# Adaptive layer norm, state-space mixing and routed feed-forward on one core: setup reordered, the weight fetches put one behind the other, the router's bias added on VectorE

## The reference

```
h   = layernorm(x) * (1 + ca) + sa
S_t = a * S_(t-1) + (1 - a) * h_t                # a = sigmoid(decay_logit), per channel
x   = x + ga * (S @ W.T + b + conv5(h) + conv_b)
h   = layernorm(x) * (1 + cb) + sb
logits = gelu(h[last token] @ Wp1 + bp1) @ Wp2 + bp2
e   = argmax(softmax(logits))                    # one of 8 experts for the whole row
x   = x + gb * (h + 0.3 * ((gelu(h @ W1[e] + b1[e]) @ W2[e] + b2[e]) @ Wo + bo))
```

## Time and profile before

| | us |
|---|---|
| median of 3 runs | 666.33 (662.33 to 667.11) |
| the profiled execution | 664.8 |
| its span, first to last instruction | 662.8 |
| PE busy | 640.0 (97% of the span) |
| DVE busy | 561.0 (85%) |
| ACT busy | 562.2 (85%) |
| POOL busy | 447.6 (68%) |
| TensorE's mean granted clock | 0.996 of full |

### The profile page before, as it was taken

One profiled execution on the slowest core, in us unless ns is written; L12 is line 12 of the kernel. 1 busy time (PEld: TensorE's weight loads), 2 busy tenths in 40 slices (PEclk: granted clock), 3 DMA queues, 4 the chain that ended last, 5 costly groups with the idle time before them and its releaser, 6 DMA issues.

```text
span 662.8 us, 11162 instructions
## 1 busy us (share of the span) xinstructions
PE 640.0 (97%) x3469; PEld 526.8 (79%) x3469; DVE 561.0 (85%) x863; ACT 562.2 (85%) x976; POOL 447.6 (68%) x536
## 2 busy tenths in 40 slices
PE   6988999999999999999999999999999999999986
PEld 6877778888888878888888888888888878888765
DVE  1697889999999989999999999999999989998612
ACT  3788688889988888888998889888899889887753
POOL 2885476876667666777676766778776766666543
PEclk9999999999999999999999999999999999999999
DMA  8999546665555554665454555566555445555551
GB/s 288 357 349 319 162 128 192 191 186 149 156 159 180 159 183 167 192 192 179 124 194 149 182 161 186 164 191 191 189 143 153 150 167 188 160 159 159 159 158 65
DMA packets 55454, 120.58 MB, mean 182 GB/s; under 512 B 5643, under 2 KB 43364, under 8 KB 46180
## 3 DMA queue, kind: packets, MB, share of 16 engines
q1 hardware_dynamic: 51844, 115.65, 54.9%
q10 hardware_dynamic: 3552, 4.23, 2.1%
HBM read 61.12 MB, written 25.19 MB: 130 GB/s over the span
## 4 chain that ended last, share of the span: by engine, by line
PE 82%; DMA 8%; ACT 3%; DVE 3%; issue 2%; POOL 1%; SPq 1%; DVEq 0%; ACTq 0%
PE U L1051 10%; PE U L1053 8%; PE U L1052 8%; PE Q L1071 8%; PE TR L1091 8%; PE Q L1066 8%; PE Q L1067 8%; DMA up_w<-up_table 5%; PE Q L1083 4%; PE Y L1035 4%; PE Y L1031 4%; PE Y L1032 4%; PE TR L1083 4%; PE Q L1016 2%; DMA xr<-in_L_ffn_W_dram 2%
## 5 line engine op out<-in xcount | busy, mean ns | idle before, releaser
L454 POOL TENSOR_TENSOR g_lo<-g,g_hi 128x512 fp32r<-128x512 f32 x128 | 169.8, 1329 | 151.5 <-ACT g_hi L614 149.4
L835 DVE SCALAR_TENSOR_TENSOR Y<-h,taps,Y 128x512 f32<-128x512 f32 x320 | 222.4, 750 | 3.2 <-PE Y L1035 0.9
L1051 PE MATMUL U<-hid_hi,up_w 128*128 128x512 f32 x256 | 110.1, 430 | 4.7 <-DMA up_w<-up_table 3.7
L1066 PE MATMUL Q<-g_hi,down_w 128*128 128x512 f32 x256 | 103.7, 405 | 0.3 <-issue 0.3
L566 ACT ACTIVATE S<-xr,nmr,rstd 128x256 f32<-128x256 f32 x128 | 66.6, 591 | 42.2 <-POOL S_lo L462 40.0
L1067 PE MATMUL Q<-g_hi,down_w 128*128 128x512 f32 x256 | 101.1, 395 | 0.0
L1053 PE MATMUL U<-hid_lo,up_w 128*128 128x512 f32 x256 | 100.8, 394 | 0.0
L1052 PE MATMUL U<-hid_hi,up_w 128*128 128x512 f32 x256 | 100.6, 393 | 0.0
L783 DVE BATCH_NORM_STATS2 st<-xr 128x6 f32<-128x512 f32 x128 | 88.0, 709 | 12.8 <-DMA xr<-in_L_attn_x_dram 8.5
L880 DVE TENSOR_TENSOR_SCAN S<-keep,h 128x512 f32<-128x512 f32 x64 | 76.6, 1235 | 25.3 <-ACT h L684 25.3
L607 ACT ACTIVATE g<-U,up_w 128x512 f32<-128x512 f32 x128 | 87.2, 682 | 10.8 <-PE U L1053 10.3
(11 more groups left out here) (116 smaller groups left out, 1272.3 us busy)
## 6 DMA issues: line engine op xcount, KB each, us to landing
up_w<-up_table SPq DMA_DIRECT2D x32, 1027.0 KB, 6.6
down_w<-down_tab SPq DMA_DIRECT2D x32, 1024.0 KB, 8.6
xr<-in_L_attn_x_dram SPq DMA_DIRECT2D x32, 512.0 KB, 3.5
out_dram<-xr SPq DMA_DIRECT2D x64, 256.0 KB, 2.3
xr<-in_L_ffn_W_dram ACTq DMA_DIRECT2D x5, 512.0 KB, 10.2
xr<-in_L_ffn_W_dram SPq DMA_DIRECT2D x4, 512.0 KB, 8.9
up_table<-g_lo SPq DMA_DIRECT2D x2, 1024.0 KB, 11.8
up_table<-down_w SPq DMA_DIRECT2D x2, 1024.0 KB, 13.4
```

The source lines that it names most:

```text
L454: nc.gpsimd.tensor_tensor(g_lo[:, f], g[:, f % 2], g_hi[:, f].bitcast(f32), ALU.subtract).then_inc(g_lo_ready, 1)
L835: ins = nc.vector.scalar_tensor_tensor(out=Y[c][:, :], in0=h[:, c, k:k + T], scalar=taps[:, c, k:k + 1], in1=Y[c][:, :], op0=ALU.mult, op1 ...
L1051: mm(U[f % 2][:, :], up_w[:, par, UP + w:UP + w + P], hid_hi[:, par, c], start=(c == 0), stop=False)
L1066: mm(Q[c][:, :], down_w[:, par, 1, w:w + P], g_hi[:, f], start=(f == 0), stop=False)
```

## The change

1. The router's bias leaves TensorE: `router_logits` is a single product, and VectorE adds the bias from PSUM into a new tile `logits`, with a wait of its own, before `max` and `max_index`.
2. In `fetch`, SyncE waits until `up_w` has landed before it issues `down_w`.
3. In TensorE's slot, `to_channels(i + 3)` moves ahead of `router_logits(i + 1)`, and `down(i, 1)` moves ahead of `up(i, 3)`.
4. ScalarE's slot has `gelu(i, 1)` ahead of `g_high(i, 0)`, and `g_high(i, 3)`, `s_high(i + 3, 0)`, `s_high(i + 3, 1)`, `gate2(i)` in this order at its end. GpSimd's has `gate_beta(i)` first.
5. All five setup lists are put in another order. SyncE no longer waits there for the modulation weights, and issues W2[0] and W ahead of the first x.

```diff
--- before.py
+++ after.py
@@ fetch, on SyncE
                 if r == 0:
                     sp.wait_ge(s_down_lo, 2 * E)
+
+                sp.wait_ge(up_loaded[par], 16 * (r // 2 + 1))
                 sp.dma_start(down_w[:, par].rearrange("p k n -> p (k n)").bitcast(f32),
@@ setup, on SyncE
             def prologue():
                 vectors()
+                load_w2(0)
+                load_w()
                 load_x(0)
-                load_w2(0)
+                load_wo()
                 load_taps()
-
-                for_modulations()
+                load_router()
                 load_w1(0)
...
                 split_out(3)
+                split_out(4)
+                beta_out()
...
@@ router, on VectorE
             def router(r):
                 dve.wait_ge(r_logits, r + 1)
-                nc.vector.max(top8[:, :], U[1][0:1, 8:8 + E]).then_inc(top_ready, 1)
+                if r == 0:
+                    dve.wait_ge(s_small, SMALL_LOADED)
+                nc.vector.tensor_tensor(logits[:, :], U[1][0:1, 8:8 + E], bp2_sb[:, :], ALU.add).then_inc(logits_ready, 1)
+                dve.wait_ge(logits_ready, r + 1)
+                nc.vector.max(top8[:, :], logits[:, :]).then_inc(top_ready, 1)
                 dve.wait_ge(top_ready, r + 1)
-                nc.vector.max_index(sel8[:, r % 2], top8[:, :], U[1][0:1, 8:8 + E]).then_inc(sel_ready, 1)
+                nc.vector.max_index(sel8[:, r % 2], top8[:, :], logits[:, :]).then_inc(sel_ready, 1)
@@ slot, on ScalarE
                 if row(i):
                     gelu(i, 0)
+                    gelu(i, 1)
                     g_high(i, 0)
-                    gelu(i, 1)
                     g_high(i, 1)
@@ router_logits, on TensorE
                 pe.wait_ge(nav_ready, r + 1)
-                mm(U[1][0:1, 8:8 + E], nav[:, :], wp2[:, :], start=True, stop=False)
-                mm(U[1][0:1, 8:8 + E], ident[0:1, 0:1], bp2_sb[:, :], start=False, stop=True).then_inc(r_logits, 1)
+                mm(U[1][0:1, 8:8 + E], nav[:, :], wp2[:, :], start=True, stop=True).then_inc(r_logits, 1)
@@ slot, on TensorE
                     up(i, 2, (1,))
+                if row(i + 3):
+                    to_channels(i + 3, xn1, xn1_ready, t1_done)
                 if row(i + 1):
                     router_logits(i + 1)
-                if row(i + 3):
-                    to_channels(i + 3, xn1, xn1_ready, t1_done)
                 if row(i):
+                    down(i, 1)
                     up(i, 3)
                 if row(i + 2):
                     back_to_tokens(i + 2)
                 if row(i):
-                    down(i, 1)
                     down(i, 2)
                     down(i, 3)
```

More of the change, by code:

```diff
@@ L119, in adaln_attention_ffn_kernel @@
         nav = sb("nav", [P, 1])
+        logits = sb("logits", [1, E])
         top8 = sb("top8", [1, 8])
@@ L312, in vectors @@
                     sp.dma_start(dst, src).then_inc(s_vecs, 16)
-            def for_modulations():
-                for n in range(NMOD - 1):
-                    sp.wait_ge(s_wmod[n], 16 * DC)
             def load_w():
@@ L687, in prologue @@
             def prologue():
+                w2T_copy(0)
                 xn1_of(0)
                 w1_hi(0)
-                w2T_copy(0)
-                w1_hi(1)
-                mix_high()
                 h_of(0)
                 down_high(0, 0)
+                down_high(0, 1)
+                mix_high()
                 w2T_copy(1)
                 s_high(0, 0)
-                down_high(0, 1)
+                s_high(0, 1)
+                w1_hi(1)
+                down_high(1, 0)
                 w1_hi(2)
+                xn1_of(1)
+                w2T_copy(2)
                 w1_hi(3)
[L700 to L703, removed]
                 down_high(1, 1)
                 w1_hi(4)
-                w1_hi(5)
[L707 to L713, removed]
+                w2T_copy(3)
+                down_high(2, 0)
+                h_of(1)
+                down_high(2, 1)
+                gate1(0)
+                s_high(1, 0)
+                w2T_copy(4)
+                down_high(3, 0)
+                w1_hi(5)
+                w1_hi(6)
+                down_high(3, 1)
                 s_high(1, 1)
-                w2T_copy(4)
-                w1_hi(6)
                 w2T_copy(5)
-                down_high(3, 1)
+                xn1_of(2)
                 down_high(4, 0)
-                xn1_of(2)
-                w1_hi(7)
                 xn2_of(0)
@@ L725, in prologue @@
                 w2T_copy(6)
+                w1_hi(7)
                 down_high(5, 0)
-                hid_high(0)
[L728 to L735, removed]
-                down_high(6, 1)
+                gate1(1)
+                h_of(2)
+                down_high(5, 1)
+                w2T_copy(7)
+                down_high(6, 0)
+                down_high(6, 1)
+                nav_of(0)
+                s_high(2, 0)
+                s_high(2, 1)
+                hid_high(0)
                 down_high(7, 0)
@@ L910, in prologue @@
                 down_low(3, 1)
+                conv(1, 0, 6)
                 down_low(4, 0)
-                conv(1, 0, 6)
                 down_low(4, 1)
                 conv(1, 6, 10)
+                down_low(5, 0)
+                down_low(5, 1)
                 scan(2, 0)
-                down_low(5, 0)
                 scan(2, 1)
+                stats1(3)
+                down_low(6, 0)
+                down_low(6, 1)
+                router(0)
                 residual1(1, 0)
-                down_low(5, 1)
-                down_low(6, 0)
-                stats1(3)
-                router(0)
-                down_low(6, 1)
                 residual1(1, 1)
+                s_low1(2)
                 down_low(7, 0)
                 down_low(7, 1)
-                s_low1(2)
             def slot(i):
```

79 lines of the change are left out of this document (37 added, 42 removed).

## The result

The changed kernel took 683.92 us (median of 4 runs, 683.06 to 684.94) against 665.2 us for the kernel before (662.33 to 667.11): ratio 1.030, 95% interval 1.026 to 1.033. It is 3% slower, outside the range of the prediction and on its other side. The profiled execution has a span of 681.3 us (before 662.8), its mean granted clock 0.999 of full speed.

What follows compares the result with a forecast made beforehand. TensorE was taken as the bound; 7.5 + 0.5 + 1.4 + 1.8 + 0 + 0.7 - 0.4 = 11.5 us off the profiled 664.8 gave 653.3, moved half way toward the median's 1.5 us excess: 654 us, range 645 to 663.

Steps and rivals of the forecast that it cites:

- The step that failed: Steady slot: TensorE, busy all 18.40 us, sets its length; VectorE, with 1.3 us to spare, is next.
- The slower rival: `g_lo` of `up(i, 3)` comes late in every slot, 0.70 us of wait each; 674 us, chance 0.09.
- 4.7 us to spare: GpSimd's spare time in a steady slot, given as the argument against `g_lo` coming late.
- Bias and transposes, 0.25 us a slot: TensorE between `up(i, 2)` and the next large matmul: saving of 0.13 to 0.42 us, taken as 0.25.
- The term of 7.5 us: Bias product and moved transposes over all slots: 29 x 0.25 + 2 x 0.13 us saved, range 3.9 to 12.4.
- the first rival: VectorE becomes the bound; slot stays 18.4 us, 661 or 662 us in all, chance 0.15.
- Index: TensorE's two waits for the router's index go, as six matmuls now stand in between: gain 0.5 us.
- Fetch, 1.4 + 1.8 us: `up_w` lands some 1.7 us earlier: 1.4 us of waits in the middle saved, 1.8 in the tail.
- Setup, 0: Reordered setup lists gain nothing: `down(0, 0)` starts at 80.1 against 79.96.
- its wait of 0.70: Slot 0: TensorE's wait for `g_lo` goes, since TensorE stands still before and the others catch up; gain 0.7 us.
- Clock: Slot 0: 0.4 us taken off for the chance that TensorE's pauses make the granted clock fall.

Runs made afterwards that it cites:

- e2: Kernel before with only `gelu(i, 1)` moved ahead of `g_high(i, 0)`: 688.2 us, ratio 1.037.
- e9: Kernel before with 0.54 us of unused extra work on GpSimd ahead of `norm1` in each slot: 688.6 us, ratio 1.035.
- f7: Changed kernel with each slot's scans replaced by multiply-adds reading one operand from SBUF, one from PSUM (computes something else): 659.2 us, ratio 0.993.
- e3: Changed kernel with TensorE's slot back in the old order: 684.0 us, ratio 1.029.
- e7: Kernel before with only the router's bias moved to VectorE: 669.2 us, ratio 1.007.
- e6: Kernel before with only the wait of `down_w`'s fetch for `up_w` added: 661.5 us, ratio 0.995.
- f3: Kernel before with the fetch wait and all of the change's reordered setup: 660.0 us, ratio 0.995.
- e4: Changed kernel with `norm1(i + 4)` moved behind `g_low(i, 2)` on GpSimd: 701.0 us, ratio 1.056.
- f1: Changed kernel with row i + 4's statistics and `norm1` moved to the start of the slot: 686.3 us, ratio 1.034.
- f4: Kernel before with the fetch wait, and row i + 4's statistics and `norm1` moved to the start of the slot: 679.1 us, ratio 1.022.
- f8: f3 with only the power of `norm1` left on GpSimd, its other instructions on VectorE: 670.0 us, ratio 1.010.
- f5: Changed kernel with only the power of `norm1` left on GpSimd, its other instructions in the slots on VectorE: 660.4 us, ratio 0.995.

## Why the prediction was wrong

**The step that failed** is the first one: "a slot lasts as long as its TensorE instructions take to start one after the other", carried over to a slot of 18.15 us with the lengths of GpSimd's and VectorE's instructions unchanged. GpSimd's slack was read as time it could be late by. It was not that: in the trace of before, the negation of `norm1` passed ahead of the scan by 0.21 us, and where it does not, the instructions do not keep their lengths. The trace of the kernel before had the whole collision in it. In slot 0 the scan starts ahead of the negation (84.89 against 85.10):

```profile
85.10 1.04 POOL L438 TENSOR_SCALAR nmr<-st 128x4 f32<-128x4 f32 x1
86.11 1.96 POOL L440 TENSOR_TENSOR rstd<-rstd,minus_half 128x4 f32<-128x4 f32 x1
```

The wait of 0.70 us for `g_lo` and the slot of 19.41 us come behind it. The page had the power as a mean of 1193 ns for the group; taken one by one, it lasts 1.04 or about 2.0 us.

**The slower rival** had the sign (674 us; measured 684), the wait (line 1075, each slot, 0.55 us where it took 0.70) and even the edit, `gelu(i, 1)` ahead of `g_high(i, 0)`. Place and cause were wrong: it is the `g_lo` of `up(i, 2)`, and what makes it late is not the shorter cover ahead of `down(i, 3)` but the collision. So "4.7 us to spare" was taken as a reason against it and it got 0.09. e2 and e9 show how little that reason weighs. That the size came out near was luck: the 0.70 us were taken from slot 0, whose wait was this same collision, which the rival did not name.

**Bias and transposes, 0.25 us a slot.** Right at the spot: from the last matmul of `up(i, 2)` to `down(i, 1)` it is now about 1.32 us instead of 1.56. But the transposes did not get shorter behind the large matmul (294.15 to 295.12, 0.97 us; before 0.98), and why they take longer than the 0.79 us of `back_to_tokens` no run shows; the gain is the bias's product and the 0.1 us for `nav`. And of 0.24 only about 0.05 is left where the collision is gone (f7, 18.35 against 18.40). The mix takes the rest: 2.90 us from its start to the next `up` in f7, 2.75 before. `back_to_tokens` begins later, so do `residual1` and VectorE's half of `S_lo`, for which TensorE's loads now wait, in f7:

```profile
PEld Y L1049 <- DVE S_lo L851: 10.2, 31, 1.4
```

That wait was to show the first rival, which so took its part. The term of 7.5 us is worth about 1.5 (29 x 0.05), less than its lower end, which by its own terms is 4.0 and not 3.9.

**Index.** The waits for it are gone in the change, as forecast, since `down(i, 1)` stands between. e3 and e7 show what it costs without: 12.8 us of TensorE's loads waiting in 29 slots.

**Fetch, 1.4 + 1.8 us.** The sum is right: 3.1 us in e6. Its two terms miss in opposite directions. In the traces the two long slots in the middle give back 1.9 us and the last one 1.0 (16.27 to 15.28). `down_w` later cost nothing but at row 0, where `down(0, 0)` starts at 80.59 in e6 and at 79.96 before. The Trainium skill, "SBUF — State Buffer", section "The DMA setup-cost knee", gave 4.4 us for each by estimate; the trace has 4.9 and 4.8.

**Setup, 0.** Right (f3 against e6, the same ratio). In the change `up(0, 0)` started at 75.66 against 75.44, and `down(0, 0)` at 81.19 where 80.1 was forecast. That slot 0 would lose its wait of 0.70 was right too: it is 18.26 us where it was 19.41. That the others catch up while TensorE stands still, the reason given for it, no run tested. What the trace shows is that the wait was the collision: in slot 0 the negation now starts ahead of the scan (85.43 against 85.60), and in the later slots it does not.

**Clock.** 0.999 over the span: the 0.4 us were not spent.

## What to carry to other kernels

Before an order is changed beside a bound engine, compare the lengths of one and the same instruction over the whole trace on the engines that have slack. Where a small one has two lengths, find what stands beside the long one, and how close the short one comes to it. Then find which of the collisions reaches the engine that bounds: here one of about 1 us on GpSimd was covered and one of 1.7 us was not. The distance to that one, not the idle time of the engine, is the margin. When a fix moves the work away, ask what the moved piece now holds up: e4, f1, f4 and f8 all took the collision away and lost more, or as much, to a wait that was not there before.

## What the runs showed of the hardware

A small instruction of GpSimd that starts while VectorE's scan runs is held up: on 128x4 numbers 0.23 us became 1.02 and ended with the scan, and 1.04 became 1.96 and ended 0.83 us behind it (change, at 296.14 and 297.14). One that starts ahead of the scan is not (0.24 us at 295.83, against the scan at 295.92). An instruction of VectorE that is no scan but has two operands in the SBUF does the same (`S_lo`, 1.30 to 1.75 us in the change), and one that reads one operand from the PSUM does not (f7, 0.23 and 1.04).

It goes the other way too. VectorE's product of two operands of 128x4 in the SBUF, begun during `g_lo`, took 1.17 to 1.20 us in f5 and f8 and ended 0.02 us behind `g_lo` in all 56 slots; how long it takes alone no trace shows. VectorE's half of `S_lo` takes 0.67 us alone (f8) and took 1.21 when begun during GpSimd's half (before, at 275.81). But a scan that begins 0.02 us behind the power is not held: it took 1.25 us (before, at 270.36) where the first scan of a pair otherwise takes 1.23, while the power went on for 1.04.

The Trainium skill, "SBUF — State Buffer", section "Who interferes with whom", states this: "A DVE instruction with two SBUF inputs contends with a GpSimd instruction that reads SBUF", and it calls the ports that the two share an exclusive lock. The runs agree in both directions, but for the scan behind the power, which did not wait for its end. That rule, weighed against the 0.21 us by which the negation passed ahead of the scan, was the one that spoke against this change.
